# A fused attention and mixture-of-experts kernel: GpSimd adds up three of the four key chunks' exponentials, the ones products are regrouped, and GpSimd's row sends stand two slots apart

## The chip, the cores and the metric

The kernel runs on one core of a Trainium2 chip, as one launch. The metric is the device time of one execution, in microseconds (us). Five engines work beside each other, each through its own list of instructions in order: TensorE (PE; PEld are its weight loads), VectorE (DVE), ScalarE (ACT), GpSimd (POOL) and SyncE (SP), which issues most DMAs. They meet only in semaphores and in DMAs.

## What is computed

Two layers on x of 16 batches x 256 rows x 512 positions. The first is a small attention block and a low-rank routed linear layer; the second is an attention with 8 heads and a mixture of 64 experts. The change lies in the second layer's attention:

```python
def _L1_xattn_ref(q, k, v, gamma):            # q = layernorm(x), k = v = ctx
    qh = q.reshape(B, h, dq, Lq)              # h = 8 heads, dq = 32, Lq = Lk = 512
    kh = k.reshape(B, h, dq, Lk)
    vh = v.reshape(B, h, dv, Lk)
    qk = jnp.einsum('bhdq,bhdl->bhql', qh, kh) * scale
    sm = jax.nn.softmax(qk, axis=-1)
    ret = jnp.einsum('bhql,bhdl->bhdq', sm, vh)
    return gamma * ret.reshape(B, Dv, Lq)
x = x + _L1_xattn_ref(_layernorm(x), ctx, ctx, gamma)
x = x + _L1_ffn_ref(_layernorm(x), ...)       # 64 experts, each row goes to 8 of them
```

The softmax needs, for each head and query, the sum of its 512 exponentials over the keys.

## The kernel before

**Slots.** The order of all work up to the experts is written out by hand. Time is counted in slots, 32 to a batch; tables (`TENSOR`, `SCALAR`, `VECTOR`, `GPSIMD`, `SYNC` and their `_OUT` and `_TAIL` companions) give each step a slot, and `schedule` sorts them into one list for each engine. A table's number is a place in that list, not a time: a slot lasts as long as its work. While batch b is in the second layer's attention, the first layer of batch b+1 (the `prep` steps) and the routing of batch b-1 (the `disp` steps) stand between its slots. I call the 32 slots of a batch a period; there are 16.

**Attention.** Four heads make a quad, two quads a batch, 32 in all. A quad has four steps, one for each chunk of 128 keys, and a step has four slots, one for each head. In slot n PE multiplies keys and queries (L686), ACT takes the exponentials into `p_t` (L956), four heads side by side, and PE also makes the scores for a slot 20 ahead (L677), from which DVE takes maxima (L1192). After a step, PE multiplies its four heads of `p_t` by the values (L698, `weighted`). `p_t` has two buffers, so the exponentials of a step wait until everything that reads the step two before has read it.

**Sums.** A product with a matrix of ones sums over the 128 keys of a chunk. GpSimd adds the first two chunks into `p_sum` (L1442, `add_weights`, 4 adds of 128x512 for a quad). PE then makes three groups of ones products for a quad: `sums0` on `p_sum` (L713), `sums2` on the third chunk and `sums1` on the fourth (both L720), each four matmuls of 32 columns. ACT inverts the sums through a logarithm and an exponential (L968, L972), DVE scales the weighted sum (L1208) and adds it to x (L1214).

**The first layer's chain.** After its last product with `prob_t` (L613) a batch goes through short steps on several engines: ACT copies the latent (L897), DVE takes its moments (L1098, L1100), PE the mean (L620), DVE the variance (L1104), GpSimd its reciprocal root (L1414, L1416, the step `lat_rstd` at slot 25), DVE scales (L1109, L1113), ACT clips (L900), PE multiplies by `out_w` (L628), DVE adds and takes moments (L1123, L1076), GpSimd again a reciprocal root (L1371 to L1379, `rstd2` at slot 28.75), ACT normalizes (L853), PE transposes (L634, slots 33 and 34.25, that is 1 and 2.25 of the next period). All engines keep their order, so one that waits here holds back the attention behind it.

**Sends.** After routing (DVE to `slot_i`, L1290), GpSimd scatters the rows of a batch into `slot_rows` with 16 indirect DMAs (L1454, `send`). The experts' loop starts when all sends have landed.

## Time and profile before

| | us |
|---|---|
| median of 3 runs | 1804.5 |
| lowest and highest | 1799.24 and 1807.82 |
| span of the profiled execution | 1799.6 |
| attention with first layer and routing, first to last exponential in the profile | 103.6 to 1130.3 |
| experts' loop, from the first load of its rows | 1200.1 to the end |

No other time than its span is given for the profiled execution; the span lies 4.9 us under the median and inside the runs. The profile has the busy time of each engine, groups of instructions by line with what ended the idle time ahead of them, the chain of waits followed back from the end, and the instructions in order of time. "remote" as a releaser is a semaphore event that the profile can't put down to an instruction.

### The profile page before, as it was taken

The page shows a single profiled execution, that of the slowest core. Times are in us where ns is not written, and L with a number is a line of the kernel's source. Part 1 is how long each engine was busy: PE and PEld are TensorE (multiplying, and loading weights), DVE is VectorE, ACT ScalarE, POOL GpSimd, SP SyncE. Part 2 cuts the span into 40 slices and gives each one's busy share as a digit, 9 for nine tenths or more (in the row PEclk, how much of TensorE's full clock was granted, in tenths as well). Part 3 has the DMA queues.
Part 4 walks back from the last instruction along what each step waited for, and adds up shares of the span by engine and source line. Part 5 has one row for each costly group of instructions (what it writes and reads, how often), then busy time and mean ns, then how long its engine had stood idle before and what let it go on. Part 6 is the DMA issues. An engine that isn't in the chain of part 4 may idle for free.

```text
span 1799.6 us, 25136 instructions
## 1 busy us (share of the span) xinstructions
PE 1593.1 (89%) x8144; PEld 1022.0 (57%) x8144; DVE 1191.2 (66%) x2674; ACT 971.3 (54%) x1938; POOL 953.5 (53%) x889
## 2 busy tenths in 40 slices
PE   5799999989999999999999988329998999999995
PEld 2444454444454454444444443229987888888884
DVE  2477778767767877877877865217765767666652
ACT  3345665655655665665665635115554555555552
POOL 4122326455464455455455446556666666666665
PEclk8889999999999999999999989659999999999997
DMA  9957654363363363352342230059999999999995
GB/s 330 303 150 254 229 144 129 121 187 112 124 210 110 116 193 103 101 168 84 89 136 65 58 99 23 21 182 245 253 255 245 254 258 247 255 250 268 245 237 82
DMA packets 148337, 311.91 MB, mean 173 GB/s; under 512 B 27674, under 2 KB 37786, under 8 KB 148208
## 3 DMA queue, kind: packets, MB, share of 16 engines
q1 hardware_dynamic: 109296, 238.89, 42.8%
q0 software_dynamic: 38912, 71.43, 18.1%
q8 instruction: 65, 1.06, 0.2%
q14 instruction: 64, 0.52, 0.1%
HBM read 141.25 MB, written 155.91 MB: 165 GB/s over the span
## 4 chain that ended last, share of the span: by engine, by line
PE 46%; DMA 20%; issue 12%; DVE 10%; another core or an unknown queue 3%; SPq 3%; ACT 3%; POOL 2%; DVEq 1%; POOLq 0%; ACTq 0%
DMA out_rows<-y_slots,row_ids 18%; PE bank L686 7%; PE bank L698 6%; PE bank L677 5%; PE bank L655 3%; PE bank L720 3%; PE bank L600 2%; DVE max_col L1192 2%; SPq L484 2%; PE bank L613 2%; PE bank L606 2%; PE bank L628 2%; POOL out_rows L1501 2%; PE bank L739 1%
## 5 line engine op out<-in xcount | busy, mean ns | idle before, releaser
L1192 DVE TENSOR_REDUCE max_col<-bank 128x1 f32<-128x512 f32 x512 | 340.2, 682 | 148.8 <-PE bank L677 142.0
L956 ACT ACTIVATE p_t<-bank 128x512 f32<-128x512 f32 x512 | 294.3, 596 | 206.7 <-PE bank L686 183.3
L1501 POOL DMA_INDIRECT out_rows<-y_slots,row_ids x128 | 222.6, 1739 | 203.3 <-DMA out_rows<-y_slots,row_ids 160.9
L1454 POOL DMA_INDIRECT slot_rows<-row,slot_i x256 | 255.0, 996 | 77.6 <-issue 76.9
L686 PE MATMUL bank<-q_stack,k_stack 98*128 98x512 f32 x512 | 277.1, 544 | 4.9 <-ACT p_t L956 4.1
L1442 POOL TENSOR_TENSOR p_sum<-p_t 128x512 f32<-128x512 f32 x128 | 168.3, 1320 | 195.9 <-ACT p_t L956 194.0
L677 PE MATMUL bank<-k_stack,q_stack 96*128 96x512 f32 x512 | 212.9, 417 | 4.6 <-DVE max_col L1192 4.3
L686 PEld LDWEIGHTS bank<-q_stack,k_stack 98*128 98x128 f32 x512 | 97.6, 192 | 191.4 <-issue 163.3
L1491 POOL TENSOR_TENSOR down_lo<-down,down_hi 96x1024 fp32r<-96x1024 f32 x64 | 188.4, 2944 | 15.3 <-DVE down_hi L1350 15.3
L1319 DVE TENSOR_TENSOR x_slots_t_lo<-bank,x_slots_t_hi 128x512 fp32r<-128x512 f32 x128 | 88.3, 690 | 160.6 <-ACT x_slots_t_hi L1008 160.6
L795 PE MATMUL bank<-gate_up_hi,x_slots_t_hi 128*128 128x384 f32 x512 | 186.1, 364 | 0.6 <-DVE x_slots_t_lo L1319 0.5
L796 PE MATMUL bank<-gate_up_lo,x_slots_t_hi 128*128 128x384 f32 x512 | 174.6, 341 | 0.0
L797 PE MATMUL bank<-gate_up_hi,x_slots_t_lo 128*128 128x384 f32 x512 | 174.5, 341 | 0.0
L1028 ACT ACTIVATE y_slots<-bank,x_slots 128x512 f32<-128x512 f32 x128 | 88.1, 688 | 128.3 <-PE bank L819 125.3
L1340 DVE TENSOR_TENSOR gate_up_lo<-gate_up,gate_up_hi 128x768 fp32r<-128x768 f32 x128 | 142.7, 1116 | 7.2 <-issue 7.2
L698 PE MATMUL bank<-p_t,v_t 128*32 128x512 f32 x1024 | 140.7, 622 | 0.2 <-DVE head_sb L1208 0.2
L784 PE MATMUL bank<-ident,x_slots 128*128 128x128 f32 x512 | 80.7, 281 | 66.1 <-DMA x_slots<-slot_rows 65.8
L655 PE MATMUL bank<-base_w,x_t 128*128 128x512 f32 x256 | 129.8, 620 | 0.0
L677 PEld LDWEIGHTS bank<-k_stack,q_stack 96*128 96x128 f32 x512 | 99.0, 194 | 53.0 <-issue 29.3
L1371 POOL TENSOR_SCALAR row_rstd<-row_mv 128x2 f32<-128x2 f32 x48 | 10.9, 228 | 199.3 <-DVE row_mv L1078 199.3
L784 PEld LDWEIGHTS bank<-ident,x_slots 128*128 128x128 f32 x512 | 62.9, 143 | 91.1 <-DMA x_slots<-slot_rows 40.0
L1038 ACT CAST gate_up_hi<-gate_up 128x768 fp32r<-128x768 f32 x128 | 105.4, 824 | 13.4 <-DMA down<-in_down 13.4
(178 smaller groups left out, 3246.5 us busy)
## 6 DMA issues: line engine op xcount, KB each, us to landing
gate_up<-in_gate_up SPq DMA_DIRECT2D x64, 768.0 KB
slot_rows<-row SPq DMA_DIRECT2D x64, 577.0 KB, 8.0
x_slots<-slot_rows SPq DMA_DIRECT2D x64, 577.0 KB
k_stack<-prob SPq DMA_DIRECT2D x192, 128.0 KB, 3.8
down<-in_down SPq DMA_DIRECT2D x64, 384.0 KB
q_stack<-x_t SPq DMA_DIRECT2D x128, 128.0 KB
x<-in_x SPq DMA_DIRECT2D x16, 512.0 KB, 3.6
ctx<-in_ctx SPq DMA_DIRECT2D x16, 512.0 KB, 4.5
```

The costliest lines, as they stand in the source:

```text
L655: e.matmul(bank[:, :], x_t[:, k, c, :], base_w[:, c, :], start=c == 0, stop=False)
L677: e.matmul(psum[2 + n % 2][:, :], q_st[b % 2][0:SK, head, c * P:(c + 1) * P], k_st[b % 2][0:SK, head, :], start=True, stop=True).then_inc( ...
L686: e.matmul(psum[n % 2][:, :], k_st[b % 2][0:SKM, head, j * P:(j + 1) * P], q_st[b % 2][0:SKM, head, :], start=True, stop=True).then_inc(fu ...
L698: m = e.matmul(psum[4][h * DQ:(h + 1) * DQ, :], v_t[b % 2][:, j, head + h, :], p_t[step % 2][:, h, :], start=j == 0, stop=j == C - 1)
L795: e.matmul(bk[:, 0:2 * INNER], xt_hi[u % 3][:, c, :], gu_hi[nw][:, c, :], start=c == 0, stop=False)
L796: e.matmul(bk[:, 0:2 * INNER], xt_hi[u % 3][:, c, :], gu_lo[nw][:, c, :], start=False, stop=False)
L797: m = e.matmul(bk[:, 0:2 * INNER], xt_lo[u % 3][:, c, :], gu_hi[nw][:, c, :], start=False, stop=c == C - 1)
L956: e.activation(p_t[step % 2][:, h, :], psum[n % 2][:, :], ACT.Exp, scale=SCALE).then_inc(free[n % 2], 1)
L1192: e.tensor_reduce(max_col[quad % 2][:, h, c:c + 1], psum[2 + n % 2][:, :], X, ALU.max, negate=True).then_inc(free[2 + n % 2], 1)
L1454: e.indirect_dma_start(out=slots_dram, in_=rows[b % 2][:, k, :], in_offset=None, out_offset=bass.IndirectOffsetOnAxis(ap=slot_i[b % 2][:, ...
L1491: e.tensor_tensor(dn_lo[nw][:, :, :], dn[i][:, :, :], dn_hi[nw][:, :, :].bitcast(F32), ALU.subtract).then_inc(dn_lo_ok, 1)
L1501: e.indirect_dma_start(out=out, out_offset=bass.IndirectOffsetOnAxis(ap=row_ids[e_ % NI][:, q, :].bitcast(U32), axis=0), in_=ye[e_ % NY][: ...
```

## The change

Three things, with no change to data or to the other tables:

- GpSimd adds the third chunk too: 4 more adds of 128x512 for a quad (p_sum + p_t), in the four slots behind the first four. `sums2` is gone. What waited for `sums2` to have read `p_t` now waits for the add.
- `sums0` and `sums1` both stand at slot 2.5 of the next quad (16 slots to a quad), just ahead of the last `weighted` of theirs at 2.75. Before they stood at -4 and 0.25, and `sums2` at -3.5. ACT's and DVE's steps behind them move from 0.75, 2.75, 4 and 5.5 to 3.75, 4.25, 5 and 6.
- The 16 sends of a batch go from slots 63, 64, ... 78 to 49.5, 51.5, ... 79.5.

```diff
-GPSIMD_OUT = {"rstd": 14.25, "send": 63}
+GPSIMD_OUT = {"rstd": 14.25, "send": 49.5}
-TENSOR_TAIL = {"sums0": -4, "sums2": -3.5, "sums1": 0.25}
-SCALAR_TAIL = {"sums": 0.75, "expand": 2.75}
-VECTOR_TAIL = {"inv": 4, "add": 5.5}
+TENSOR_TAIL = {"sums0": 2.5, "sums1": 2.5}
+SCALAR_TAIL = {"sums": 3.75, "expand": 4.25}
+VECTOR_TAIL = {"inv": 5, "add": 6}
+SEND_STEP = 2
...
-        if "add" in core and n // H4 % C == 1:
+        if "add" in core and n // H4 % C in (1, 2):
             out.append((n + 1, 2, ("add", n)))
...
                 elif what == "sums0":
-                    w.wait_ge(p_sum_ok, H4 * (quad + 1))
+                    w.wait_ge(p_sum_ok, 2 * H4 * (quad + 1))
...
-                    if j < 2:
-                        w.wait_ge(p_sum_ok, H4 * quad + h + 1)
-                    elif j == C - 2:
-                        w.wait_ge(sums_mid, quad + 1)
+                    if j < C - 1:
+                        w.wait_ge(p_sum_ok, H4 * (2 * quad + j // 2) + h + 1)
                     else:
                         made("tail", "sums", quad)
...
-                e.tensor_tensor(p_sum[:, h, :], p_t[(step - 1) % 2][:, h, :], p_t[step % 2][:, h, :],
-                                ALU.add).then_inc(p_sum_ok, 1)
+                if j == 1:
+                    w.wait_ge(free[(n - H4) % 2], (n - H4) // 2 + 1)
+                    w.wait_ge(p_sum_read, quad)
+                    before = p_t[(step - 1) % 2]
+                else:
+                    w.wait_ge(p_sum_ok, H4 * (2 * quad) + h + 1)
+                    before = p_sum
+                e.tensor_tensor(p_sum[:, h, :], before[:, h, :], p_t[step % 2][:, h, :], ALU.add).then_inc(p_sum_ok, 1)
```

**GpSimd, second quad of a period.** `lat_var` is DVE's variance of the first layer's chain, the two rows that write `lat_all` are `lat_rstd`, the row that waits for `row_moments` begins `rstd2`. Before:

```order
L1442 TENSOR_TENSOR p_sum<-p_t 128x512 [waits p_sum_read,bank_free0]
L1442 TENSOR_TENSOR p_sum<-p_t 128x512 [waits bank_free1]
L1442 TENSOR_TENSOR p_sum<-p_t 128x512 [waits bank_free0]
L1442 TENSOR_TENSOR p_sum<-p_t 128x512 [waits bank_free1]
L1414 TENSOR_SCALAR lat_all<-lat_all 128x1 [waits lat_var]
L1416 TENSOR_TENSOR lat_all<-lat_all,neg_half 128x1 [waits pool_step]
L1371 TENSOR_SCALAR row_rstd<-row_mv 128x2 [waits xn4_ok,row_moments]
```

The same place after the change:

```order
L1445 TENSOR_TENSOR p_sum<-p_t 128x512 [waits p_sum_read,bank_free0]
L1456 DMA slot_rows<-row,slot_i 16384x577
L1445 TENSOR_TENSOR p_sum<-p_t 128x512 [waits bank_free1]
L1445 TENSOR_TENSOR p_sum<-p_t 128x512 [waits bank_free0]
L1456 DMA slot_rows<-row,slot_i 16384x577
L1445 TENSOR_TENSOR p_sum<-p_t 128x512 [waits bank_free1]
L1445 TENSOR_TENSOR p_sum<-p_sum,p_t 128x512 [waits p_sum_ok,bank_free0]
L1412 TENSOR_SCALAR lat_all<-lat_all 128x1 [waits lat_var]
L1414 TENSOR_TENSOR lat_all<-lat_all,neg_half 128x1 [waits pool_step]
L1456 DMA slot_rows<-row,slot_i 16384x577
L1445 TENSOR_TENSOR p_sum<-p_sum,p_t 128x512 [waits p_sum_ok,bank_free1]
L1445 TENSOR_TENSOR p_sum<-p_sum,p_t 128x512 [waits p_sum_ok,bank_free0]
```

`lat_rstd` now stands behind five adds and two sends where it stood behind four adds, and one send, two adds, another send and a last add follow it ahead of `rstd2`.

**PE, around the products with `out_w` (L628) of the same chain.** L713 and L720 are the ones products. Before:

```order
L686 MATMUL bank<-q_stack,k_stack 128x512 [waits bank_free0]
L677 MATMUL bank<-k_stack,q_stack 128x512 [waits bank_free2]
L713 MATMUL bank<-p_sum,ones 32x512 [waits p_sum_ok,bank_free6]
L713 MATMUL bank<-p_sum,ones 32x512 x3
L709 MATMUL bank<-ident,max_col 16x128 [waits bank_free3,bank_free5]
L628 MATMUL bank<-theta,out_w 128x512 [waits bank_free7,lat_relu]
L628 MATMUL bank<-theta,out_w 128x512 [waits bank_free5]
L720 MATMUL bank<-p_t,ones 32x512 [waits bank_free1]
L720 MATMUL bank<-p_t,ones 32x512 x3
L686 MATMUL bank<-q_stack,k_stack 128x512
```

After:

```order
L686 MATMUL bank<-q_stack,k_stack 128x512 [waits bank_free0]
L677 MATMUL bank<-k_stack,q_stack 128x512 [waits bank_free2]
L709 MATMUL bank<-ident,max_col 16x128 [waits bank_free3,bank_free7]
L628 MATMUL bank<-theta,out_w 128x512 [waits bank_free6,lat_relu]
L628 MATMUL bank<-theta,out_w 128x512 [waits bank_free5]
L686 MATMUL bank<-q_stack,k_stack 128x512 [waits bank_free1]
```

Both groups have left this place; the third group of the quad stood a few rows on, still ahead of the transposes (L634).

**PE, behind the second transpose (L634) and ahead of the low-rank products (L642).** After the change:

```order
L634 MATMUL bank<-ident,xn 128x128 [waits bank_free5,xn2_ok]
L634 MATMUL bank<-ident,xn 128x128 x3
L713 MATMUL bank<-p_sum,ones 32x512 [waits p_sum_ok,bank_free6]
L713 MATMUL bank<-p_sum,ones 32x512 x3
L720 MATMUL bank<-p_t,ones 32x512 x4
L698 MATMUL bank<-p_t,v_t 32x512 x4
```

Before, L698 followed the transposes at once; the quad's two groups now stand here.

## Rows read from the trace of the kernel before

**Rows 1.** The page: span, busy time of each engine.

```profile
span 1799.6 us, 25136 instructions
PE 1593.1 (89%) x8144; PEld 1022.0 (57%) x8144; DVE 1191.2 (66%) x2674; ACT 971.3 (54%) x1938; POOL 953.5 (53%) x889
```

**Rows 2.** Groups by line: count | busy us, mean ns | idle before, releasers.

```profile
L1454 POOL DMA_INDIRECT slot_rows<-row,slot_i x256 | 255.0, 996 | 77.6 <-issue 76.9 <-DVE slot_i L1290 0.8
L1442 POOL TENSOR_TENSOR p_sum<-p_t 128x512 f32<-128x512 f32 x128 | 168.3, 1320 | 195.9 <-ACT p_t L956 194.0
L720 PE MATMUL bank<-p_t,ones 128*32 128x512 f32 x512 | 69.1, 611 | 3.8 <-ACT p_t L956 3.0 <-issue 0.8
L713 PE MATMUL bank<-p_sum,ones 128*32 128x512 f32 x256 | 34.1, 604 | 0.4 <-POOL p_sum L1442 0.3
```

**Rows 3.** The chain of waits in one period: start us, us, what.

```profile
554.53 0.99 PE bank L713 x8
...
561.93 1.04 PE bank L720 x8
```

**Rows 4.** Busy time in stretches: stretch, length, PE, PEld, DVE, ACT, POOL, clock, DMA.

```profile
546.00:564.50 18.50, 18.16 (x93) 7.74 (x92) 17.07 (x30) 10.13 (x19) 9.19 (x12) 1.00 0.04 16
529.00:534.00 5.00, 2.23 (x16) 0.94 (x13) 1.91 (x11) 1.97 (x4) 1.45 (x2) 1.00 1.00 342
534.00:538.00 4.00, 4.00 (x20) 1.96 (x18) 2.39 (x8) 2.26 (x4) 0.94 (x2) 0.57 0.48 150
```

**Rows 5.** In order of time, the first layer's chain in one period: start, us, instruction.

```profile
547.76 0.69 ACT L897 ACTIVATE theta<-bank,lat_b 128x512 f32<-128x512 f32 x1 [0.49 <-PE bank L613]
...
552.24 0.19 POOL L1414 TENSOR_SCALAR lat_all<-lat_all 128x1 f32<-128x1 f32 x1 [0.62 <-DVE lat_all L1104]
...
554.83 0.63 ACT L900 ACTIVATE theta<-theta 128x512 f32<-128x512 f32 x1
...
560.18 0.22 POOL L1371 TENSOR_SCALAR row_rstd<-row_mv 128x2 f32<-128x2 f32 x1 [7.11 <-DVE row_mv L1078]
...
563.00 0.81 ACT L853 ACTIVATE xn<-x,row_off,row_rstd 128x512 f32<-128x512 f32 x1
...
564.40 0.60 PE L634 MATMUL bank<-ident,xn 128*128 128x128 f32 x4
```

**Rows 6.** GpSimd in order of time: adds in that period, adds and sends in turn later.

```profile
546.06 2.62 POOL L1442 TENSOR_TENSOR p_sum<-p_t 128x512 f32<-128x512 f32 x2 [10.85 <-ACT p_t L956]
549.01 2.61 POOL L1442 TENSOR_TENSOR p_sum<-p_t 128x512 f32<-128x512 f32 x2 [0.32 <-ACT p_t L956]
...
1098.58 1.29 POOL L1442 TENSOR_TENSOR p_sum<-p_t 128x512 f32<-128x512 f32 x1
...
1101.05 1.29 POOL L1442 TENSOR_TENSOR p_sum<-p_t 128x512 f32<-128x512 f32 x1
```

**Rows 7.** ACT and PE at the end of a first quad: two single instructions, then waits.

```profile
257.28 0.25 ACT L963 CAST max_hi<-bank 16x128 fp32r<-16x128 f32 x1 [0.37 <-PE bank L709]
531.84 0.25 ACT L963 CAST max_hi<-bank 16x128 fp32r<-16x128 f32 x1 [3.35 <-remote]
...
ACT max_hi L963 <- remote: 17.4, 6, 3.5
PE bank L606 <- ACT prob L890: 15.1, 7, 2.9
```

**Rows 8.** Two DVE lines: min/median/max ns, first and last start.

```profile
L1214 DVE TENSOR_TENSOR x<-x,head_sb x32: 658/692/1735, 148.2 to 1135.0; 128x512 f32<-128x512 f32 x32
L1240 DVE TENSOR_SCALAR r_max<-r_max x16: 169/896/1789, 250.7 to 1162.3; 128x2 f32<-128x2 f32 x16
```

**Rows 9.** DVE and GpSimd in order of time, between attention and experts.

```profile
1148.34 0.29 DVE L1238 TENSOR_REDUCE r_max<-bank 128x2 f32<-128x128 f32 x1 [12.66 <-remote]
...
1155.73 1.28 POOL L1454 DMA_INDIRECT slot_rows<-row,slot_i  x1 [0.76 <-DVE slot_i L1290]
...
1197.81 0.97 POOL L1454 DMA_INDIRECT slot_rows<-row,slot_i  x1 [0.30 <-issue]
```

More of the change, by code:

```diff
@@ L115, in schedule @@
             for n in range(HALF * dims["TOPK"] if what == "send" else 1):
-                out.append((SLOTS * (b + 1) + o + n, 5, ("disp", b, what, n)))
+                out.append((SLOTS * (b + 1) + o + n * SEND_STEP, 5, ("disp", b, what, n)))
     return [(at, ev) for at, _, ev in sorted(out, key=lambda x: x[:2])]
@@ L254, in build @@
         p_sum_read = sem("p_sum_read")
-        sums_mid = sem("sums_mid")
         rows_ok = sem("rows_ok")
@@ L714, in finish_quad @@
                     m.then_inc(p_sum_read, 1)
-                elif what in ("sums2", "sums1"):
-                    step = C * quad + (C - 2 if what == "sums2" else C - 1)
+                elif what == "sums1":
+                    step = C * quad + C - 1
                     w.wait_ge(free[0], H4 // 2 * (step + 1))
@@ L720, in finish_quad @@
                         m = e.matmul(bank[h * DQ:(h + 1) * DQ, :], ones[:, 0:DQ], p_t[step % 2][:, h, :], start=False,
-                                     stop=what == "sums1")
-                    m.then_inc(done if what == "sums1" else sums_mid, 1)
+                                     stop=True)
+                    m.then_inc(done, 1)
             def dispatch(b, what, _):
@@ L1437, in add_weights @@
                 step, h = divmod(n, H4)
-                quad = step // C
-                w.wait_ge(free[(n - H4) % 2], (n - H4) // 2 + 1)
+                quad, j = divmod(step, C)
                 w.wait_ge(free[n % 2], n // 2 + 1)
-                w.wait_ge(p_sum_read, quad)
-                e.tensor_tensor(p_sum[:, h, :], p_t[(step - 1) % 2][:, h, :], p_t[step % 2][:, h, :],
-                                ALU.add).then_inc(p_sum_ok, 1)
+                if j == 1:
[6 more added lines that the diff above has]
+                e.tensor_tensor(p_sum[:, h, :], before[:, h, :], p_t[step % 2][:, h, :], ALU.add).then_inc(p_sum_ok, 1)
             def dispatch(b, what, place=0):
```

## The prediction

> **What bounds the kernel now.** I read the page first [rows 1]: PE is busy 89% of the span, the other engines 53% to 66%. PE busy is no peak, so I went on to the stretches [rows 4]. From 546.0 to 564.5, most of a second quad, PE is busy 18.16 of 18.5 us: attention runs at PE's pace, and each ones product is paid for. The chain of waits says the same: three groups of ones products lie on it in that stretch, the first at 0.99 and the third at 1.04 us [rows 3]. Then I looked at how long PE could go faster there, in order of time [rows 5]. The first layer's chain starts with ACT's copy at 547.76, and PE's second transpose, which ends it, starts at 564.40, 16.64 us later. Its input, ACT's second L853, ends at 563.81, only 0.59 us ahead. So **this stretch has two bounds 0.5 us apart**: PE's work, and a chain of short steps that goes through GpSimd twice (552.24 and 560.18). The reader is to see that GpSimd stood idle ahead of both: 0.62 us, until DVE's variance was there, and 7.11 us. It is 53% busy, yet it answers at once just here. The same chain stands in 15 periods (the last has no first layer beside it); I found its steps at the same distances in each from the third on.
>
> **What the change removes.** One of three ones groups of a quad: 32 groups. L720 has 512 matmuls in 69.1 us, or 64 groups of 1.08 us, and L713 32 groups of 1.07 us [rows 2]; on the chain one is worth 1.0 us. Were PE alone the bound, that would be 32 us off.
>
> **What it moves, and the stretch of the chain (B).** From ACT's copy (L897) to the second transpose PE had three ones groups, 3.0 us; all of them leave it. The order shows the quad's groups behind the second transpose. PE's work in B falls from 16.6 to 13.6 us, and the chain becomes the bound: at best B falls by the 0.5 us of slack.
>
> But the chain grows. `lat_rstd` stood behind four adds, which GpSimd ran at 546.06 to 551.62 [rows 6]. Now two sends stand among them and a fifth add behind them. From one add to the next with a send between is 2.47 us (1098.58 to 1101.05), without one 1.31 us (2.62 for two) [rows 6]. From 546.06: add, send, 548.53; add, 549.84; add, send, 552.31; add, 553.62; add, 554.93. Then `lat_rstd`, at 552.24 before, starts at 554.95, **2.7 us later**. The exponential that the fifth add needs is one slot behind the fourth add's, and that add ended by 551.62, so it is there. Behind it stand a send, two adds, a send and an add: from 555.8, when `lat_rstd` is done (it takes some 0.8 us), 1.15 + 1.3 + 1.3 + 1.15 + 1.3 = 6.2 us, to 562.0. `rstd2` was due at 560.18 and is now due 2.7 us later, 562.9, so it isn't held a second time; 0.9 us are left. What is queued behind GpSimd's late answer is DVE's scaling, ACT's clip and, at L628, PE with all keys and scores behind it. B becomes 16.6 - 0.5 + 2.7 = 18.8 us: **+2.2 us in a period**. With sends from the third period on these are 13 periods, 28.6 us. In the first two there are no sends: five adds instead of four, of which the last would end 1.3 us past 551.62, at 552.9, 0.7 us past the old start of `lat_rstd`; with 0.5 us of slack +0.2, in all 0.4 us. Bounds for B: if the adds fall 0.7 us earlier, +1.5; if DVE's scaling also waits for an add, +3.5; 20 to 46 us over 13 periods.
>
> **The rest of a period (A).** From the second transpose to the next copy PE had three groups, all of the first quad. Now it has four: two of the quad before, two of its own. PE is busy there but for two places (below), so +1.0 us in 15 periods, +15.0. Both new groups at slot 2.5 stand ahead of the low-rank products, whose results start another chain, so they don't fill the wait that follows it. Bounds: 0, if they did, and 16.
>
> **The place where PE's results come late.** At the end of a first quad ACT's copy of the maxima waits 3.35 us at 531.84 for a semaphore, though PE's product is recorded as long done; without sends, at 257.28, it waits 0.37 us [rows 7]. PE then stands: 2.77 of 5 us idle at 529 to 534, and the granted clock is 0.57 of full in the 4 us behind, so the lower of its levels (1.2 GHz against 2.4) for most of them [rows 4]. PE waited 15.1 us for L890 in seven periods, and ACT's copy 17.4 us in six for something unnamed [rows 7]. The trace has it only in periods with sends, while four or more sends run one after another. The change puts an add or a gap between sends there. I take it that this goes: -15.1 us and, for the clock, 4 periods at (1 - 0.57) x 4 = 1.7 us, -7: **-22 us**. Bounds: 0 and -22. The Trainium skill (SBUF — State Buffer, Who interferes with whom) says that PE and ACT never wait for a port that GpSimd uses; by that a burst of sends isn't held to block PE through SBUF, the rows don't say what else does, and the term would be 0.
>
> **DVE beside more adds.** L1214 takes 0.66 us at least and 1.735 at most, with a median of 0.69 [rows 8]; the long ones are those that start inside an add; L1240, 0.17 us at best, has a median of 0.90 us, beside GpSimd's other adds [rows 8]. So some DVE instructions wait for an add to end. Adds now run through eight slots of each quad, in the first quad across the routing's short instructions, on whose `mask` PE waits at slot 12. One such wait a period that PE sees, 0.7 us, and some of the 0.74 us by which `inv` now stands ahead of x's second statistics: 0.8 us x 12 = **+10 us**; bounds 0 and 25. The Trainium skill (same page and section) says that a VectorE instruction with two SBUF inputs waits for the whole of a GpSimd instruction that reads SBUF, and that reductions don't. The rows agree for L1214; by the rule each of some ten routing instructions might wait, nearer to 25 than to 10.
>
> **Sends and the end.** Sends cost GpSimd 1.0 us each and about 0.3 between [rows 2, 9]; their number stays. Behind the attention the 16 sends of one batch ran first, DVE got PE's routing product only at 1148.34 after 12.66 us, and the 32 of the last two batches ran from 1155.73 to 1198.8 before the experts could load [rows 9]. Now 8 of the 16 are done earlier, but the last quad's 8 adds and 4 sends take 8 x 1.3 + 4 x 1.15 = 15 us where 4 adds took 5, so its sums come some 5 us later. I take 0; bounds -10 and +5. The last send of a batch now stands one slot ahead of the DVE copy into the same rows buffer (slots 79.5 and 80.5): covered, since GpSimd runs ahead, or 2 us of DVE.
>
> **The sum.** 28.6 + 0.4 + 15.0 - 22 + 10 + 0 = +32. On the span, 1799.6 + 32 = 1831.6. The median of the runs lies 4.9 us above the span: **1836.5 us**. With its terms at their bounds this case goes from about 1812 to 1866.
>
> **Rivals.**
> 1. *GpSimd isn't late, and PE's late results go* (faster). If exponentials come earlier with PE relieved, so that the fifth add is over before DVE's variance, B gains 0.5 us: 15 x -0.5 + 15 - 22 + 0 to 5, less up to 10 at the end, is -12 to -20: 1784 to 1796, with 1789 in the middle. Against it: 5 adds and 2 sends are 8.9 us of work in a gap of 6.2 us. It decides if GpSimd reaches `lat_rstd` within 0.5 us of DVE's variance.
> 2. *PE's late results stay and DVE's waits are dear* (slower still): 29 + 15 + 0 + 25 = +69: 1873. For it: no row shows the cause of the late results.
> 3. *The terms cancel*: B at its low bound, DVE at 0, the end at -10: 20 + 15 - 22 - 10 = +3: 1807. Each is possible, all together less so.
> 4. *PE is the only bound*: -32 - 22 = -54: 1750. Against it the 0.59 us [rows 5].
>
> **How the numbers follow.** Chances: my forecast 0.62, rival 1 0.14, rival 2 0.11, rival 3 0.10, rival 4 0.03. A measurement of this kernel tells about 0.5%, 9 us, from no change. Faster is rivals 1 and 4: 0.17. Within 0.5% is rival 3: 0.10. Slower is the rest: 0.73. For 8 in 10 the range goes from 1797, between rivals 1 and 3, to 1866.
>
> **What the profile would show.** Right: `lat_rstd` waits no longer for DVE, but starts at the end of an add, some 2.7 us later behind ACT's copy; PE idle ahead of L628 and L634, 4 to 5 us in a period; L713 and L720 each 32 groups; from ACT's copy to the second transpose 18 to 20 us instead of 16.64. ACT's copy of the maxima waits under 1 us. Wrong: if that distance stays under 16.7 us the forecast falls, and most of all if GpSimd still waits for DVE ahead of `lat_rstd`; if ACT still waits 3 us at the maxima, rival 2. If the distance grows and the time doesn't, the gain is in A, where I saw PE as full.

## The result: slower, by four times what was forecast

| | before | after |
|---|---|---|
| median of 4 runs, us | 1803.66 | 1942.22 |
| lowest and highest | 1799.24 and 1807.82 | 1938.58 and 1943.75 |
| ratio after/before, 95% interval | | 1.0771 (1.0738 to 1.0804) |

The change costs 139 us. The forecast was +32 us, 1836.5, with a range to 1866: the sign was right, the size far off. First the page of the changed kernel, the lines that answer [rows 1].

```profile
span 1942.0 us, 24928 instructions
PE 1643.7 (85%) x7888; PEld 1063.3 (55%) x7888; DVE 1283.8 (66%) x2674; ACT 973.8 (50%) x1938; POOL 1123.6 (58%) x1017
```

PE has 256 instructions fewer and is busy 51 us more. The groups by line show that this isn't the ones products, of which there are now 64 groups of 8, as planned (they answer [rows 2]):

```profile
L1456 POOL DMA_INDIRECT slot_rows<-row,slot_i x256 | 268.9, 1050 | 98.2 <-issue 60.2 <-DVE slot_i L1288 34.2 <-POOL p_sum L1445 3.1
L1445 POOL TENSOR_TENSOR p_sum<-p_t 128x512 f32<-128x512 f32 x128 | 165.6, 1302 | 198.5 <-ACT p_t L954 197.6
L1445 POOL TENSOR_TENSOR p_sum<-p_sum,p_t 128x512 f32<-128x512 f32 x128 | 164.2, 1292 | 3.0 <-ACT p_t L954 1.8
L713 PE MATMUL bank<-p_sum,ones 128*32 128x512 f32 x256 | 36.9, 650 | 4.1 <-POOL p_sum L1445 4.1
L720 PE MATMUL bank<-p_t,ones 128*32 128x512 f32 x256 | 35.3, 624 | 0.0
```

The exponentials by their line, before and after (min/median/max ns, first and last start), say where the time is: the last one starts 140 us later, so the attention holds all of it.

```profile
L956 ACT ACTIVATE p_t<-bank x512: 569/597/632, 103.6 to 1129.7; 128x512 f32<-128x512 f32 x171
```

```profile
L954 ACT ACTIVATE p_t<-bank x512: 570/597/623, 106.3 to 1270.1; 128x512 f32<-128x512 f32 x171
```

Busy time in a stretch, before, then after (columns as in [rows 4]), and in some 3-us steps of one period of after:

```profile
320.00:1080.00 760.00, 710.89 (x3528) 359.17 (x3524) 568.99 (x1417) 444.64 (x892) 387.99 (x463) 0.97 0.40 121
```

```profile
320.00:1080.00 760.00, 658.59 (x2963) 344.96 (x2963) 570.73 (x1261) 398.90 (x800) 454.50 (x496) 0.90 0.38 113
...
600.00:603.00 3.00, 1.32 (x8) 0.68 (x4) 3.00 (x2) 1.08 (x2) 2.83 (x3) 1.00 0.23 89
603.00:606.00 3.00, 2.60 (x12) 1.77 (x16) 2.93 (x7) 1.11 (x2) 2.90 (x3) 0.65 0.25 98
...
609.00:612.00 3.00, 0.03 (x1) 0.06 (x1) 3.00 (x3) 0.78 (x2) 2.83 (x3) 0.79 0.14 54
612.00:615.00 3.00, 3.00 (x6) 1.42 (x6) 1.48 (x4) 0.26 (x1) 1.40 (x2) 0.50 0.31 109
```

PE is idle 13% of the stretch instead of 6.5%, and the granted clock falls from 0.97 to 0.90: behind each stand of PE come a few us at the lower level (0.50 is 1.2 GHz of 2.4). In the same steps DVE is "busy" 3.00 of 3.00 us with two or three instructions. That is the trail. Picked rows of the timeline there, DVE, GpSimd and their neighbours, with many left out between them (start, us, instruction, idle before); they answer [rows 5]:

```profile
598.57 0.69 ACT L897 ACTIVATE theta<-bank,lat_b 128x512 f32<-128x512 f32 x1 [0.49 <-PE bank L613]
599.43 2.53 POOL L1445 TENSOR_TENSOR p_sum<-p_t 128x512 f32<-128x512 f32 x2
599.65 2.87 DVE L1212 TENSOR_TENSOR x<-x,head_sb 128x512 f32<-128x512 f32 x1
603.39 0.38 PE L620 MATMUL bank<-lat_mv,ones 128*128 128x2 f32 x2 [2.08 <-DVE lat_mv L1098]
604.61 1.33 DVE L1102 SCALAR_TENSOR_TENSOR lat_all<-lat_all 128x1 f32<-128x1 f32 x1
604.63 1.29 POOL L1445 TENSOR_TENSOR p_sum<-p_sum,p_t 128x512 f32<-128x512 f32 x1
606.03 0.19 POOL L1412 TENSOR_SCALAR lat_all<-lat_all 128x1 f32<-128x1 f32 x1
607.83 3.39 DVE L1111 SCALAR_TENSOR_TENSOR theta<-theta,lat_all,ln_beta 128x512 f32<-128x512 f32 x1
608.17 2.50 POOL L1445 TENSOR_TENSOR p_sum<-p_sum,p_t 128x512 f32<-128x512 f32 x2
611.26 0.63 ACT L900 ACTIVATE theta<-theta 128x512 f32<-128x512 f32 x1 [2.10 <-DVE theta L1111]
611.97 0.37 PE L709 MATMUL bank<-ident,max_col 128*16 128x128 f32 x1 [3.25 <-DVE max_col L1190]
621.57 0.66 PE L634 MATMUL bank<-ident,xn 128*128 128x128 f32 x4
```

Read the ends. An instruction ends at its start plus its length. DVE's x add (L1212) ends at 602.52, 0.56 us after GpSimd's two adds; its variance (L1102) ends at 605.94, with the add at 605.92; its scaling (L1111) at 611.22, 0.55 us after two adds. Each starts beside an add or just ahead of one and is over only when the adds are. PE pays twice here: 2.08 us ahead of the mean (L620), and 3.25 us ahead of L709, whose input is DVE's maxima, and they stand behind the long scaling in DVE's list. It pays once more in the rest of the period, 2.2 us for the mask (21.7 us in 10 waits at L750 from 320 to 1080). From ACT's copy to the second transpose it is 23.0 us (16.64 before). The x add, the variance, the scaling and the mask by their source (min/median/max ns):

```profile
L1212 DVE TENSOR_TENSOR x<-x,head_sb x32: 679/1318/3760, 152.8 to 1280.4; 128x512 f32<-128x512 f32 x32
L1102 DVE SCALAR_TENSOR_TENSOR lat_all<-lat_all x16: 219/1340/1347, 33.0 to 1142.9; 128x1 f32<-128x1 f32 x16
L1111 DVE SCALAR_TENSOR_TENSOR theta<-theta,lat_all,ln_beta x16: 750/3385/3402, 35.1 to 1146.1; 128x512 f32<-128x512 f32 x16
L1258 DVE TENSOR_SCALAR mask<-repl x16: 226/1314/1318, 272.7 to 1303.0; 128x128 bf16<-128x128 f32 x16
```

### The profile page after: what moved, and what is told of

It reads as the page before. It is cut to its first block and busy times, and to the rows that moved or that the text cites. A ratio compares the mean times of both kernels' runs of the same rounds, so it can differ in the third digit from the quotient of the medians.

```text
span 1942.0 us, 24928 instructions
## 1 busy us (share of the span) xinstructions
PE 1643.7 (85%) x7888; PEld 1063.3 (55%) x7888; DVE 1283.8 (66%) x2674; ACT 973.8 (50%) x1938; POOL 1123.6 (58%) x1017
## 5 line engine op out<-in xcount | busy, mean ns | idle before, releaser
L1456 POOL DMA_INDIRECT slot_rows<-row,slot_i x256 | 268.9, 1050 | 98.2 <-issue 60.2
L686 PE MATMUL bank<-q_stack,k_stack 98*128 98x512 f32 x512 | 302.4, 593 | 13.9 <-ACT p_t L954 9.9
L677 PE MATMUL bank<-k_stack,q_stack 96*128 96x512 f32 x512 | 227.9, 446 | 8.2 <-DVE max_col L1190 7.1
L686 PEld LDWEIGHTS bank<-q_stack,k_stack 98*128 98x128 f32 x512 | 107.4, 211 | 181.2 <-issue 145.4
L1445 POOL TENSOR_TENSOR p_sum<-p_sum,p_t 128x512 f32<-128x512 f32 x128 | 164.2, 1292 | 3.0 <-ACT p_t L954 1.8
L698 PE MATMUL bank<-p_t,v_t 128*32 128x512 f32 x1024 | 158.5, 695 | 3.2 <-DVE head_sb L1206 1.7
L677 PEld LDWEIGHTS bank<-k_stack,q_stack 96*128 96x128 f32 x512 | 108.2, 211 | 65.9 <-issue 35.4
L1338 DVE TENSOR_TENSOR gate_up_lo<-gate_up,gate_up_hi 128x768 fp32r<-128x768 f32 x128 | 137.0, 1071 | 7.0 <-issue 7.0
L655 PE MATMUL bank<-base_w,x_t 128*128 128x512 f32 x256 | 124.7, 599 | 0.0
L817 PE MATMUL bank<-down_hi,hidden_t_hi 96*128 96x512 f32 x256 | 111.1, 434 | 1.3 <-POOL down_lo L1493 1.3
```

Of the source, the lines that this page charges most:

```text
L677: e.matmul(psum[2 + n % 2][:, :], q_st[b % 2][0:SK, head, c * P:(c + 1) * P], k_st[b % 2][0:SK, head, :], start=True, stop=True).then_inc( ...
L686: e.matmul(psum[n % 2][:, :], k_st[b % 2][0:SKM, head, j * P:(j + 1) * P], q_st[b % 2][0:SKM, head, :], start=True, stop=True).then_inc(fu ...
L698: m = e.matmul(psum[4][h * DQ:(h + 1) * DQ, :], v_t[b % 2][:, j, head + h, :], p_t[step % 2][:, h, :], start=j == 0, stop=j == C - 1)
L1445: e.tensor_tensor(p_sum[:, h, :], before[:, h, :], p_t[step % 2][:, h, :], ALU.add).then_inc(p_sum_ok, 1)
L1456: e.indirect_dma_start(out=slots_dram, in_=rows[b % 2][:, k, :], in_offset=None, out_offset=bass.IndirectOffsetOnAxis(ap=slot_i[b % 2][:, ...
```

## The experiments

Two theories. **Theory 1**: VectorE stands until GpSimd's adds are over. No semaphore of the program makes it wait there, so the engines don't meet in semaphores and DMAs alone, as I wrote ahead of the prediction. **Theory 2**, my forecast's: GpSimd's queue makes `lat_rstd` late. To these came the ones groups' places and the sends. Lines are named as in the changed kernel (a kernel's own may differ by up to 3). The groups of runs were on different chips, and before itself took 1729 us in one group and 1804 to 1824 in the others; so kernels are compared by their ratio to the runs of before beside them, and in us only within a group.

### The change taken apart (before here: 1729 us)

**e1**, the sends alone:

```diff
-GPSIMD_OUT = {"rstd": 14.25, "send": 63}
+GPSIMD_OUT = {"rstd": 14.25, "send": 49.5}      # and SEND_STEP = 2
```

> The kernel before with the sends alone changed: first send at slot 49.5, two slots apart; adds and ones groups as before. Theory 1 (the loss comes from VectorE waiting for GpSimd's adds): the adds are those of before, so no loss; the place where PE's results come late after a run of sends goes, -10 to -25 us: 1780 to 1795. Theory 2 (the loss comes from GpSimd's queue, with sends ahead of the first layer's small steps): the sends now stand among the adds and ahead of lat_rstd, so 1 to 1.2 us a period are lost on the chain, 1815 to 1825.

Measured 1753.65, ratio 1.0159 (1.0114 to 1.0204). It is 25 us slower, which theory 1 did not expect; the late results that were to go were not there on this chip (see e3's row below). **e2**, the changed kernel with `"send": 63` and `SEND_STEP = 1`:

> The changed kernel with the sends put back (slot 63, one slot apart): the third chunk's adds and the moved ones groups alone. Theory 1 (VectorE waits for adds): the wait of L1212, L1102 and L1111 of 2.9, 1.3 and 3.4 us comes mostly from adds in pairs and stays; the stand of PE at the end of a first quad comes back: 1900 to 1960. Theory 2 (GpSimd's queue, my forecast's): without sends among the adds lat_rstd is only 0.7 us late, 1800 to 1830.

Measured 1899.08, 1.0973 (1.0927 to 1.1019). Theory 2 falls as the main cause. I had expected PE's late results to come back with the old sends. They didn't: ACT waits 0.5 us at most for the maxima in this trace. **e3**, the groups moved, none removed:

```diff
-TENSOR_TAIL = {"sums0": -4, "sums2": -3.5, "sums1": 0.25}
+TENSOR_TAIL = {"sums2": -3.5, "sums0": 2.5, "sums1": 2.5}    # ACT's and DVE's tails as in the change
```

> The kernel before with its three ones groups, of which the first and the third now stand at 2.5 behind the quad's end and the second stays at -3.5: nothing is removed, adds and sends are as before. Theory 1 (VectorE waits for adds): no add is new, so within 15 us of before, 1790 to 1820. The forecast's step on the two stretches (two groups leave the stretch of the chain, which gains at most 0.5 us, and 2.1 us fall into the rest): +1.6 x 15 = +24 us, 1828. If putting the groups elsewhere were the whole loss: 1900 or more.

Measured 1766.7, 1.0225 (1.0178 to 1.0273): 38 us for moving two groups, above both estimates. **e4** leaves the third chunk out and writes instead:

```diff
-                e.tensor_tensor(p_sum[:, h, :], before[:, h, :], p_t[step % 2][:, h, :], ALU.add)
+                    e.memset(blank[:, :], 0.0)      # third chunk only; 128x1420 bf16
```

> The changed kernel in which the third chunk's 128 adds are replaced by as many memsets of 1420 columns on GpSimd, about 1.3 us each, at the same places and waits (the third chunk of exponentials is thus left out of the sums). GpSimd is as busy and its queue as long, but reads nothing there. Theory 1 (VectorE waits while an add reads what it reads): L1212, L1102 and L1111 fall to about 0.7, 0.2 to 1.3 and 0.75 us, the granted clock rises from 0.90 to 0.96 or more, and the time to 1770 to 1815. Theory 2 (GpSimd's queue): no change, 1930 to 1950. If a memset blocks VectorE too: also 1930 to 1950, but with the three lines as long as in the changed kernel.

Measured 1885.77, 1.0912 (1.0868 to 1.0955), outside both forecasts. The memsets take 1.29 us each. The mask by its source:

```profile
L1259 DVE TENSOR_SCALAR mask<-repl x16: 227/1444/1448, 262.7 to 1256.1; 128x128 bf16<-128x128 f32 x16
```

A memset that reads nothing holds up the mask as an add does. The variance and the scaling are back at 0.22 and 0.75 us, but in most periods they met sends, or were over as a memset began. In the first two periods, which have no sends, the scaling did meet memsets. Here it is in e4, then at the same place in the changed kernel:

```profile
153.88 4.08 POOL L1446 MEMSET blank<- 128x1420 bf16 x3
154.76 0.75 DVE L1112 SCALAR_TENSOR_TENSOR theta<-theta,lat_all,ln_beta 128x512 f32<-128x512 f32 x1
```

```profile
159.21 1.71 POOL L1445 TENSOR_TENSOR p_sum<-p_sum,p_t 128x512 f32<-128x512 f32 x1
159.84 1.63 DVE L1111 SCALAR_TENSOR_TENSOR theta<-theta,lat_all,ln_beta 128x512 f32<-128x512 f32 x1
```

With GpSimd as busy and its queue as long, the scaling takes 0.75 us in the middle of memsets and 1.63 us beside adds, and ends 0.55 us after the add at 159.21. That add is long too, 1.71 us instead of some 1.3: here each engine waits for the other. So the wait hangs on what the GpSimd instruction does, and theory 1 holds for this line; the queue doesn't explain it. For the time e4 gives no clean price, since the mask and the x add still wait (PE's wait at L709 falls from 32.4 to 4.3 us between 320 and 1080, those for the mask and the mean stay at 26.4 and 20.8).

### Without the third chunk's adds (before: 1806 us)

> The kernel before, unchanged, for its trace on the chip of this group of runs. The spacing of the sends alone had cost 25 us and the moved groups alone 38 us against runs of before at 1729 us, 75 us shorter than in the profiled execution of before; if that one is long because of the place where PE's results come late, ACT's copy of the maxima waits under 1 us here in every period; if not, it waits 3 us here too, and some other wait is shorter.

> The changed kernel, unchanged, on the chip of this group of runs. All theories: 1.1 times before or more (the adds alone were 1.097 times before). If effects of adds, sends and groups simply add up: 1.10 to 1.13 times before.

After, 1939.65, is 1.0737 (1.0655 to 1.0819) times before, under the 1.10 or more that I expected from e1 to e3 on the other chip: the effects don't add up. ACT's wait for the maxima, in before here and in e3, which has the same sends:

```profile
ACT max_hi L963 <- remote: 14.1, 5, 3.5
```

```profile
ACT max_hi L963 <- PE bank L709: 4.6, 12, 0.4
```

PE's late results are there, and absent in e3, where before took 1729. The two chips differ in this. **e5** has a memset of one column in each third add's place, **e6** 13 of them:

```diff
-                    e.memset(blank[:, :], 0.0)
+                    e.memset(blank[:, 0:1], 0.0)
```

> The changed kernel in which each of the third chunk's 128 adds is replaced by a memset of one column, about 0.1 us, at the same place and with the same waits (the third chunk of exponentials is left out of the sums). All else of the change stays: one ones group fewer, the others moved, the sends two slots apart. Both theories of the adds (VectorE waits for them, GpSimd's queue is longer): they take 130 us or more away from the changed kernel, down to 1.00 to 1.04 times before. If the moved groups and the spacing were the larger part: above 1.05 times before.

> The changed kernel in which each of the third chunk's adds is replaced by 13 memsets of one column each, about 0.1 us apiece and 1.3 us together: GpSimd is busy as long as with an add, but in small pieces (the third chunk of exponentials is left out of the sums). Theory 1 (VectorE waits for the end of a GpSimd instruction): a wait is at most about 0.1 us, so L1102, L1111 and L1258 return to 0.3, 0.8 and 0.3 us and the time is within 30 us of the kernel with one memset of one column. Theory 2 (GpSimd's queue): it is as long as with the adds or with the long memsets, 1.08 times before or more.

Measured 1858.78 (1.0281) and 1852.54 (1.0245). The mask in e5:

```profile
L1259 DVE TENSOR_SCALAR mask<-repl x16: 226/226/289, 259.6 to 1219.6; 128x128 bf16<-128x128 f32 x16
```

The third chunk's adds are worth 81 us (1939.65 - 1858.78), where I had expected 130 or more. e6 was built on a wrong size, as its timeline shows:

```profile
570.34 0.45 POOL L1447 MEMSET blank<- 128x1 bf16 x13
```

13 pieces take 0.45 us together, not 1.3, since they overlap. So e6 shortens the queue too and doesn't decide between the theories. And 53 us are left with no new add at all.

### Moving the waits (before: 1808 us)

**e7** and **e8**: the changed kernel, and e5, with the x add ahead of the next quad's adds.

```diff
-VECTOR_TAIL = {"inv": 5, "add": 6}
+VECTOR_TAIL = {"inv": 4.5, "add": 4.75}
```

> The changed kernel with DVE's two steps behind a quad's sums (L1206 and L1212) at 4.5 and 4.75 instead of 5 and 6, ahead of the next quad's adds. Theory 1 (VectorE waits for adds, of the second chunk too): L1212 falls from 2.87 to about 0.7 us in second quads, the statistics behind it come 2 us sooner, PE's wait for the mean (2.1 us a period) goes, and with the clock behind it 25 to 50 us of the changed kernel's time: 1.045 to 1.065 times before where the changed kernel is 1.074. Rival (the third chunk's adds are all of it, this wait is hidden by the next one): within 10 us of the changed kernel.

> The changed kernel with the third chunk's adds replaced by memsets of one column (the third chunk is left out of the sums) and with L1206 and L1212 at 4.5 and 4.75: no new add, and the x add out of the way of the old ones. Theory 1: what was left over before (52 us with the adds replaced alone) was mostly this wait; 0.995 to 1.015 times before. Rival (the moved ones groups and the sends cost the rest): 1.02 or more.

Measured 1904.41 (1.0518; 1.0465 to 1.0571) and 1849.68 (1.0206; 1.0150 to 1.0262). e7 came as theory 1 said: the x add takes 0.69 us and PE's wait for the mean is gone. e8 came as its rival said: moving the x add didn't take away what e5 had left. On this chip the third chunk's adds are worth 55 us (e7 to e8), not 81. e7 in order of time:

```profile
591.38 0.22 DVE L1102 SCALAR_TENSOR_TENSOR lat_all<-lat_all 128x1 f32<-128x1 f32 x1
...
593.91 1.28 POOL L1445 TENSOR_TENSOR p_sum<-p_sum,p_t 128x512 f32<-128x512 f32 x1
...
595.27 0.19 POOL L1412 TENSOR_SCALAR lat_all<-lat_all 128x1 f32<-128x1 f32 x1
...
598.44 0.37 PE L709 MATMUL bank<-ident,max_col 128*16 128x128 f32 x1 [4.49 <-DVE max_col L1190]
```

Now DVE's variance is there at 591.60 and GpSimd comes to it at 595.27, 3.7 us later, behind a send and two adds: theory 2's wait, which the longer waits of theory 1 had hidden. DVE's maxima stand behind the scaling that waits for it, and PE stands 4.5 us. The two mechanisms take each other's place. **e9** does all adds, the third chunk's in quiet places:

```diff
+            late = n % H4 + 4.6 if n % SLOTS < QUAD else 2.5 + n % H4 / 2
+            out.append((n // H4 * H4 + late, 2, ("add", n)))
+                        w.wait_ge(mask_ok, b - 1)       # first quad of a batch, first add
+                        w.wait_ge(lat_scaled, b + 3)    # second quad
```

> The changed kernel complete, with its third chunk's adds where no VectorE step on the path should meet them: in a batch's first quad behind the mask (L1258), 3.6 slots later, in the second behind the first layer's scaling (L1111), between it and rstd2; L1206 and L1212 at 4.5 and 4.75. Theory 1: nearly all of the loss goes though GpSimd does all the adds: 0.99 to 1.03 times before, with the granted clock at 0.96 or more. Rival (GpSimd has no room for 128 more adds, rstd2 and the sends come late): above 1.05.

Measured 1877.57, 1.037 (1.0319 to 1.0421), 27 us less than e7 at the same GpSimd work, and 28 us over e8, which has no third adds. Its mask and scaling wait for nothing:

```profile
L1261 DVE TENSOR_SCALAR mask<-repl x16: 226/226/296, 264.6 to 1238.7; 128x128 bf16<-128x128 f32 x16
L1114 DVE SCALAR_TENSOR_TENSOR theta<-theta,lat_all,ln_beta x16: 751/752/752, 32.0 to 1082.0; 128x512 f32<-128x512 f32 x16
```

So place decides whether these instructions wait, as theory 1 says; but both numbers of the expectation were missed (clock 0.93, not 0.96). **e10** is e1's kernel again:

> The kernel before with the sends two slots apart from 49.5, alone, a second time, on the chip of this group. If before takes some 1805 us here, with PE's late results in it, the spacing takes them away: 0.975 to 0.99 times before. If before takes some 1730 us here, they are absent there and only the later lat_rstd is left: 1.01 to 1.02, as in its first run.

Measured 1771.51, 0.978 (0.9731 to 0.9828); on the chip of e1 it was 1.016. The first branch came as written; the second only told e1's run again. The same kernel is 0.038 apart on the two chips, some 68 us of 1804: if nothing else differs between them, that is what PE's late results cost. Its `lat_rstd`, rows between left out:

```profile
533.65 0.22 DVE L1105 SCALAR_TENSOR_TENSOR lat_all<-lat_all 128x1 f32<-128x1 f32 x1
534.60 1.30 POOL L1443 TENSOR_TENSOR p_sum<-p_t 128x512 f32<-128x512 f32 x1
535.98 0.19 POOL L1415 TENSOR_SCALAR lat_all<-lat_all 128x1 f32<-128x1 f32 x1
```

2.1 us late, and PE waits 1.9 us a period for it (21.0 us in 11 waits at L709).

### The queue cleared, the groups priced (before: 1824 us)

All four have the sends in new places, none between 51.5 and `lat_rstd`:

```diff
+SEND_AT = [49.5, 50.5, 51.5, 57.25, 57.75] + [59.5 + 2 * i for i in range(11)]
```

> The kernel of e8 (changed kernel, third chunk's adds replaced by memsets of one column and so left out of the sums, L1206 and L1212 early) with its sends at 49.5, 50.5, 51.5, 57.25, 57.75, 59.5 and then two slots apart: none between 51.5 and lat_rstd (57). Theory 2, GpSimd's queue, as the second bound behind VectorE's waits: lat_rstd comes 0.9 to 1.5 us behind L1102 instead of 3.6, PE's wait of 3.5 us at L709 falls below 1.5, 0.98 to 1.00 times before. Rival (the ones groups' places are what is left): within 0.5% of e8, 1.015 to 1.026.

> The kernel of e9 (all sums complete: third chunk's adds behind the mask and behind the scaling, L1206 and L1212 early) with the sends placed as in e11. If VectorE's waits and GpSimd's queue were the two causes, it comes to 1.00 to 1.02 times before, from 1.037. Rival (128 adds more are too many for GpSimd wherever they stand): no gain over e9.

> The kernel before with the sends placed as in e11, nothing else. If a late lat_rstd costs the 1.9 us that PE waits at L709 in the first spacing, this goes too: 0.955 to 0.97 times before, where the first spacing had 0.978. Rival (the chain has slack enough, or two sends behind lat_rstd make rstd2 late): 0.975 or more.

> The kernel of e13 with the first and third ones group moved to 2.5 behind the quad's end (nothing removed) and L1206 and L1212 at 4.5 and 4.75. Against e13 it gives the price of the groups' places alone: by the forecast's two stretches +1.6 us a period, 24 us, 0.97 to 0.985 times before; if the places are what is left in e8, 50 us or more over e13.

| | kernel | us | ratio (95%) |
|---|---|---|---|
| e11 | e8, sends placed | 1818.29 | 0.9998 (0.9962 to 1.0033) |
| e12 | e9, sends placed | 1895.76 | 1.0398 (1.0347 to 1.0449) |
| e13 | before, sends placed | 1743.32 | 0.9554 (0.9499 to 0.9609) |
| e14 | e13, groups moved, x add early | 1809.66 | 0.9925 (0.9888 to 0.9961) |

e11 is 0.021 better than e8: the late `lat_rstd` was some 38 us, from two chips, so good to about half of that. e12 gains nothing: with 128 adds more, what was won there is lost elsewhere (PE waits 14.8 us for the transposes' input, which it didn't in e9). **e13 beats both kernels**, by 4.5% against before; it wasn't run on the chip where before took 1729 us, and there the gain may be gone with the late results. e14 shows the price of the groups' places, 66 us over e13; DVE's x steps moved too. e3 moved the same groups with the sends at their old places and paid 38 us, so the price hangs on what else waits.

### Is the removed group worth anything (before: 1804 us)

**e15** is e13 without `sums2`; **e16** the changed kernel's sums with

```diff
-TENSOR_TAIL = {"sums0": 2.5, "sums1": 2.5}
+TENSOR_TAIL = {"sums0": 0.25, "sums1": 0.25}    # tails of ACT and DVE as before, sends as in e13
```

> The kernel of e13 (before with the sends placed) without its second ones group, 32 groups of 1.0 us, and with no add in its place: the third chunk of exponentials is left out of the sums. Nothing else moves. It shows what removing the group can bring at most. If PE alone set the pace: 32 us less than e13, 0.937 times before where e13 had 0.955. By the two bounds of the forecast (the first quad's group lies outside the chain's stretch and counts, the second quad's lies in it and gains at most its slack of 0.5 us): 15 + 8 = 23 us at most. If the chains bind nearly everywhere: under 10 us, 0.95 or more.

> The sums of the changed kernel, complete (GpSimd adds three of four chunks, one ones group less), with the two groups left both at 0.25, ahead of the second transpose, the steps behind the sums at the slots of before (inv 4, add 5.5), and the sends placed as in e13. Theory 1 (VectorE waits for adds): L1102, L1111 and L1258 are as long as in the changed kernel, 1.3, 3.4 and 1.3 us, and it is 60 to 100 us slower than the same without adds (e15). Rival (the moved groups are the larger part): within 40 us of e13.

Measured 1735.02 (0.9615; 0.9589 to 0.9641) and 1836.1 (1.0189; 1.0152 to 1.0225). One period of each, from e13, then e15, then e14:

```profile
537.40:600.30 62.90, 62.46 (x321) 31.71 (x317) 51.35 (x128) 40.29 (x82) 35.11 (x43) 1.00 0.49 148
```

```profile
536.60:599.40 62.80, 60.53 (x305) 31.40 (x301) 51.29 (x128) 40.37 (x83) 35.19 (x43) 1.00 0.48 144
```

```profile
568.60:635.10 66.50, 63.17 (x318) 32.02 (x317) 51.35 (x128) 40.13 (x82) 34.92 (x43) 1.00 0.47 140
```

In e13 PE is busy 62.46 of 62.90 us. Take two groups away and it is busy 60.53 of 62.80: **1.9 us of work gone, 0.1 us gained**; the periods on either side have the same lengths. The whole runs say the same, since e15's ratio isn't below e13's, as the third part of the expectation had it ("the chains bind nearly everywhere"). PE now waits for ACT's `prob` and DVE's maxima (e15's waits of PE from 320 to 1080: us, times, longest):

```profile
PE bank L607 <- ACT prob L891: 12.9, 11, 1.2
PE bank L678 <- DVE max_col L1191: 8.8, 14, 0.7
```

The chains run as long as PE does, in both parts of a period. In e14 PE's busy time grows by 0.7 us only, and 2.9 of the 3.6 us are new idle time: where the groups had stood there is nothing to do, where they went there was no room.

e16 against e15 is the price of the third chunk's adds once more, 101 us, with one difference more: the first group moves from -4 to 0.25. The medians of its variance and mask are 1.00 and 1.32 us. The expectation named the scaling too; it is at 0.75 us, since two sends, beside which it keeps its length, stand behind `lat_rstd`. And it is 0.063 behind e13: the least moved form of the idea loses too.

## Where the 139 us come from

From one experiment to the next, as ratios to the before beside each (chips differ, so a step between groups is good to about 0.01, 18 us), with us at 1804. The steps add up to 133 us, because after was 1.0737 beside e5 and 1.0771 in the first measurement:

| step | from, to | ratio | us |
|---|---|---|---|
| late results gone, sends placed | before, e13 | 1 to 0.9554 | -80 |
| two groups moved, x add early | e13, e14 | to 0.9925 | +67 |
| second group gone, tiny memsets in place of its adds | e14, e11 | to 0.9998 | +13 |
| sends two apart, ahead of `lat_rstd` | e11, e8 | to 1.0206 | +38 |
| x add at 6, among the adds | e8, e5 | to 1.0281 | +14 |
| third chunk's adds | e5, after | to 1.0737 | +82 |

The steps are one way through the change, and another way has other prices: the third chunk's adds cost 28 us in quiet places (e8 to e9), 55 with the x add out of their way (e8 to e7), 77 with placed sends (e11 to e12), 101 in e16. The step of the x add, +14, lies within the 0.01; in the complete kernel it is 40 (after to e7).

## Why the prediction was wrong, step by step

**Two bounds 0.5 us apart: right, and not far enough.** In B, from ACT's copy to the second transpose, they were there. But I took the rest of the period as PE's pace alone, from one stretch at 98% busy. e15 shows a second bound there too, 0.1 us behind. A busy engine says that it isn't waiting, not how much sooner the others could be. I had rival 4 (PE alone, -32) rightly at 0.03; what was missing was that no part of the 32 could come.

**B, +2.2 us a period: it was +6.4** (23.0 against 16.64), outside my bounds. `lat_rstd` starts at the end of an add, 7.46 us behind ACT's copy, where I had 4.5 + 2.7 = 7.2. That agreement is luck. The add ended at 605.92, but DVE's variance, held by two waits, ended only at 605.94, 7.37 us behind the copy, so `lat_rstd` would have been as late with an empty queue. Before, the variance ended 4.39 us behind the copy:

```profile
551.93 0.22 DVE L1104 SCALAR_TENSOR_TENSOR lat_all<-lat_all 128x1 f32<-128x1 f32 x1
```

What B had wrong is the wait: DVE's own steps wait for the adds. GpSimd's lateness alone, where nothing hid it (e11 to e8), cost some 38 us, against my 28.6.

**A, +1.0 a period, bounds to 16 us: +67 for the moved groups.** I counted the groups' 1.0 us of work and a gain of 0.5 in B. e14 shows no gain in B and new waits of PE, 2.9 us a period.

**DVE beside more adds, +10, bounds 0 and 25: this step failed most.** The third chunk's adds cost 81 us (e5) and 101 (e16) at their places, 55 where the x add was out of their way; GpSimd's longer queue is in these numbers. Two errors. I priced one wait of 0.7 us a period, from the medians of before, where adds met only instructions with slack. And I kept it apart from B, though L1102, L1111 and the mask are each on the way to PE. The Trainium skill (SBUF — State Buffer, Who interferes with whom) speaks of an exclusive lock, and says that the loser "fully blocks"; it names DVE instructions with two SBUF inputs beside a GpSimd instruction that reads, and `tensor_scalar` in the modes that use two ports. The trace agrees for both: L1111 with two inputs takes 3.39 us instead of 0.75 beside adds and 0.75 beside memsets, the mask, a `tensor_scalar` with one, 1.31 instead of 0.23 (its mode stands in no row); reductions beside adds stay at 0.69. I cited it as "nearer to 25" and then took 10.

**The clock: no term at all.** I used it to price the late results that go, and not for the 4 to 5 us of new waits that I forecast myself. One period of after has PE busy 66.6 us for the products that take 60.5 in e15, at a granted clock of 0.89 instead of 1.00. So of the 13.6 us between those periods (76.4 and 62.8), 7.5 are more idle time of PE and 6.1 go with the clock.

**Late results, -22, bounds 0 and -22: they went.** ACT's copy of the maxima no longer waits 3 us. The size was low: with the late `lat_rstd` in it the spacing alone is -36 (e10), without it -80 (e13), and e1 against e10 puts the late results at some 68. So the change won more here than I had counted, and by that estimate its costs are over 200 us where I had 54: two misses of opposite sign. I had counted PE's recorded waits in seven periods and little clock. The Trainium skill's sentence (same section) that PE and ACT never wait for a port, by which I had put the other end at 0, says nothing on what holds these results, and the runs don't either.

**Sends and the end, 0: right within 2 us.** From the start of the last exponential to the end it is 671.9 us, and 669.9 before.

**The range.** "With its terms at their bounds" doesn't give 1866: the high bounds together are 46 + 0.4 + 16 + 0 + 25 + 5 = +92, that is 1897, and the low ones 1793. The measured time lies above that too, so the sizes failed and not only their sum.

**Signs.** L713 and L720 at 32 groups each, and the maxima: right. PE idle 4 to 5 us ahead of L628 and L634: it is 5.3 us in all, but 2.1 ahead of L620 and 3.25 ahead of L709, which stands just before L628, and none at L634. Of the rivals, the second (late results stay, DVE dear) was half true; its price for DVE, 25, was too small by two to four times.

## What to carry to other kernels

Before work is moved to GpSimd, list every VectorE instruction that will run beside it and its way to the bounding engine: 1.3 us of GpSimd add can cost as much on the chain each time, up to twice that when two follow each other, and PE's clock on top. Before a product is taken off a full PE, ask what is second; here the second bound was 0.1 us behind, and 1.9 us of work bought nothing. Small moves of who stands ahead of a short step on an in-order queue were worth more than the arithmetic that was saved: 80 us in e13, PE's late results among them.

## What was not expected of the hardware

- A DVE instruction often isn't let in between two GpSimd adds that follow each other. In the first two periods it is (e4's section: 1.63 us, and the next add takes 1.71); from the third on it isn't, and what decides is open: L1111 took 3.39 us beside two adds of 1.25 us each, though its recorded start (607.83) is 0.34 us ahead of the first (608.17). The Trainium skill (SBUF — State Buffer, Who interferes with whom) gives the pair to whoever issues first; by the recorded starts the trace doesn't agree, but GpSimd's recorded spans are rough, and 0.34 us is little.
- An instruction of 128x1 waits as long as a large one (L1102, 1.34 us instead of 0.22). Beside a GpSimd memset of 1.29 us, which reads nothing, the mask took 1.44 us and the scaling its usual 0.75 (e4).
- What DVE reads decides too: L1172, also an add of 128x512 but with one input in PSUM, takes 0.69 us at most in after, beside adds and away from them. GpSimd's sends hold little: L1107 beside one stays at 0.74 us, and a `tensor_scalar` of 128x512 (L1232 in e13) takes 0.66 at most, 0.54 at least.
- PE's late results behind a run of sends are in the two traces of before, on chips where it took 1804 and 1806 us, and not in e3's, with the same sends, on the chip where before took 1729. The trace of e2, with the same sends on that chip, has none either. On the other three chips before took 1804 to 1824, so they are likely there too (not shown). Their cause is open; in every trace with the sends spaced they are gone.
- Not settled: how the adds' 81 us divide between VectorE's waits and GpSimd's queue, because each hides the other (e7). e9 gives a hint: with every add in, and the x add, variance, scaling and mask at their short lengths in most periods, it is still 28 us over e8, and PE's wait for ACT's `prob` from 320 to 1080 grows from 18.6 to 30.7 us.
